# Moving the small arithmetic of a normalisation from VectorE to GpSimd in a two-image convolution kernel

## The reference

```python
x = x + _L0_conv_ref(_gn(x))       # a two-sided cosine transform of the normalised image
x = x + _L1_conv_ref(_gn(x), ...)  # six Euler steps of an ODE

def odefunc(t, y):
    h = relu(_group_norm(y, gn1_w, gn1_b))
    h = _concat_conv(t, h, conv1_w, conv1_b)     # 3x3, 33 channels in, 32 out
    h = relu(_group_norm(h, gn2_w, gn2_b))
    h = _concat_conv(t, h, conv2_w, conv2_b)
    return _group_norm(h, gn3_w, gn3_b)
# six times: y = y + dt * odefunc(t, y)
```

## Time and profile before

| what | us |
|---|---|
| median of 3 runs | 3509.87 |
| lowest and highest | 3505.09, 3530.72 |
| the profiled execution, own time | 3496.76 |
| its span in the trace | 3494.9 |
| TensorE busy | 2976.7 |
| VectorE busy | 2722.9 |
| ScalarE busy | 2497.4 |
| GpSimd busy | 891.2 |

### The profile page before, as it was taken

How to read it: one execution, slowest core, us unless ns; L and a number is a source line. 1 busy time by engine, 2 the same in 40 slices (tenths; PEclk the granted TensorE clock), 3 DMA queues, 4 the chain that set the end, 5 groups by cost and what they waited for, 6 DMA issues and landing times.

```text
span 3494.9 us, 148263 instructions
## 1 busy us (share of the span) xinstructions
PE 2976.7 (85%) x61716; PEld 2505.7 (72%) x61716; DVE 2722.9 (78%) x6289; ACT 2497.4 (71%) x3867; POOL 891.2 (25%) x1293
## 2 busy tenths in 40 slices
PE   2599988989889998899889988889888989888884
PEld 2487777777777776777777777777776777777773
DVE  6588876887778787788877887688876887768883
ACT  0377778777786677767786776877778677787774
POOL 4034311332123221323212331133311432111111
PEclk9699999999999999999999999999999999999997
DMA  4300133113131230331314113221133113231014
GB/s 88 84 22 21 28 51 96 49 55 83 26 96 50 91 69 3 96 95 49 67 26 118 49 49 67 59 86 49 54 62 96 49 49 86 30 95 58 31 49 111
DMA packets 370208, 217.56 MB, mean 62 GB/s; under 512 B 354544, under 2 KB 354912, under 8 KB 367456
## 3 DMA queue, kind: packets, MB, share of 16 engines
q1 hardware_dynamic: 369504, 207.64, 23.7%
HBM read 104.85 MB, written 77.07 MB: 52 GB/s over the span
## 4 chain that ended last, share of the span: by engine, by line
issue 27%; PE 22%; DVE 21%; ACT 20%; POOL 4%; DMA 3%; SPq 3%; DVEq 0%; POOLq 0%; ACTq 0%
PE cps L1468 17%; ACT z L706 7%; ACT z L676 6%; DVE y L1104 3%; DVE unread_yz L1112 3%; SPq L443 2%; ACT hb L705 2%; ACT unread_z L696 2%; DVE ha L1100 2%; DVE bnt L1130 2%; PE dps L1584 2%; DMA y<-xa 2%; PE dps L1576 2%; ACT ha L705 1%; ACT y L769 1%
## 5 line engine op out<-in xcount | busy, mean ns | idle before, releaser
L1468 PE MATMUL cps<-ha,w 64*64 64x392 f16 (+1 forms) x27648 | 1373.6, 341 | 99.3 <-DVE ha L1100 68.3
L1468 PE MATMUL cps<-hb,w 64*64 64x392 f16 x27648 | 1289.8, 335 | 41.1 <-DVE hb L1100 14.6
L1468 PEld LDWEIGHTS cps<-ha,w 64*64 64x64 f16 x27648 | 1064.7, 108 | 282.5 <-issue 132.2
L676 ACT ACTIVATE z<-cps,bias_now 128x784 f32<-128x784 f32 (+2 forms) x1056 | 764.2, 739 | 652.5 <-PE cps L1468 643.0
L1468 PEld LDWEIGHTS cps<-hb,w 64*64 64x64 f16 x27648 | 1077.3, 108 | 155.6 <-issue 49.5
L513 POOL TENSOR_TENSOR small<-small,half 128x1 f32<-128x1 f32 x304 | 168.7, 555 | 1758.1 <-DVE small L1029 1224.3
L1130 DVE BATCH_NORM_STATS2 bnt<-z 128x6 f32<-128x392 f32 (+1 forms) x768 | 389.9, 551 | 149.9 <-ACT z L676 149.4
L1100 DVE TENSOR_TENSOR ha<-z,ha 128x784 f16<-128x784 f32 x384 | 383.4, 998 | 86.5 <-ACT z L706 79.2
L1100 DVE TENSOR_TENSOR hb<-z,hb 128x784 f16<-128x784 f32 x384 | 375.1, 977 | 85.7 <-ACT z L706 76.8
L706 ACT ACTIVATE z<-z,small 128x784 f32<-128x784 f32 x384 | 396.5, 1033 | 1.6
L1104 DVE SCALAR_TENSOR_TENSOR y<-z,small,y 128x784 f32<-128x784 f32 x384 | 397.6, 1038 | 0.1
(11 more groups left out here) (162 smaller groups left out, 2667.8 us busy)
## 6 DMA issues: line engine op xcount, KB each, us to landing
xa<-x_dram SPq DMA_DIRECT2D x128, 196.0 KB, 5.1
y<-xa SPq DMA_DIRECT2D x16, 1568.0 KB, 7.5
y_dram<-y SPq DMA_DIRECT2D x128, 196.0 KB, 4.7
x_dram<-x1s SPq DMA_DIRECT2D x30, 784.0 KB, 5.3
fin<-y_dram SPq DMA_DIRECT2D x30, 784.0 KB, 7.4
xs<-in_x_dram SPq DMA_DIRECT2D x116, 196.0 KB, 4.4
fin<-x_dram SPq DMA_DIRECT2D x28, 784.0 KB, 6.1
out_dram<-fin SPq DMA_DIRECT2D x28, 784.0 KB, 3.6
```

Source lines behind the costliest of these rows:

```text
L676: return nc.scalar.activation(dst, src, ACT.Identity, bias=bias_now[parts, conv:conv + 1], **more)
L1468: return pe.matmul(dst, w[hin * 64:(hin + 1) * 64, kx, a, wl, :], src[:, :, 0:NA], start=(what == "X" and n == 0), stop=(what == "Y" and n ...
```

## The change

For Z1 of both slots and all kinds of steps, ScalarE now copies the sums out of PSUM (`first_read`), and GpSimd does all small operations in `first_post`: seven, each waiting for the one before. For the next image, GpSimd does the seven operations of `next_pre` and the four of `next_post`, with ScalarE's `half_read` between. VectorE does nothing for them any more. Beside this, operations stand at other places: the batches of the next image's statistics, `last_add` (from phase 3 to behind the second product of phase 1), the first `added` (ahead of slot 1's update and not inside it), ScalarE's last activation of slot 1 (behind the last squares), and on TensorE the next image's statistics matmul, from (5, 0) to (3, 0) of phase 1, and those of Z2, from (1, 3) to (1, 5) in phase 2 and from (1, 5) to (2, 1), or to (2, 0) where the step isn't MID, in phase 3.

```diff
 POSTS = {
-    MID: [(Z1, 0), (Z1, 1), (Z2, 0), (Y, 0), (Z2, 1), (Y, 1)],
-    FOUR: [(Z1, 0), (Z1, 1), (Z2, 0), (Y, 0), (Z2, 1), (Y, 1), (IZ, 0)],
-    FIVE: [(Z1, 0), (IZ, 1), (Z1, 1), (IY, 0), (Z2, 0), (IY, 1), (Z2, 1)],
-    LAST_MID: [(Z1, 0), (Z1, 1), (Z2, 0), (Y, 0), (Z2, 1), (Y, 1)],
-    LAST: [(Z1, 0), (Z1, 1), (Z2, 0), (Z2, 1)],
+    MID: [(Z2, 0), (Y, 0), (Z2, 1), (Y, 1)],
+    FOUR: [(Z2, 0), (Y, 0), (Z2, 1), (Y, 1), (IZ, 0)],
+    FIVE: [(IZ, 1), (IY, 0), (Z2, 0), (IY, 1), (Z2, 1)],
+    LAST_MID: [(Z2, 0), (Y, 0), (Z2, 1), (Y, 1)],
+    LAST: [(Z2, 0), (Z2, 1)],
...
+            def first_post(slot, ev, n):
+
+                def at(k):
+                    return col(small, slot, Z1, k)
+
+                done = NFIRST * n
+                pool.wait_ge(stat_read, ev + 2)
+                nc.gpsimd.tensor_tensor(at(T1), at(MS), at(MS), ALU.mult).then_inc(first_done, 1)
+                pool.wait_ge(first_done, done + 1)
+                nc.gpsimd.tensor_tensor(at(VAR), at(ES), at(T1), ALU.subtract).then_inc(first_done, 1)
+                pool.wait_ge(first_done, done + 2)
+                pool.sem_inc(pool_gate, 1)
+                nc.gpsimd.tensor_scalar(at(VE), at(VAR), 0.0, gb[:, 6:7], ALU.max, ALU.add).then_inc(first_done, 1)
+                pool.wait_ge(first_done, done + 3)
+                nc.gpsimd.tensor_tensor(at(RSTD), at(VE), half[:, 0:1], ALU.pow).then_inc(first_done, 1)
+                pool.wait_ge(first_done, done + 4)
+                nc.gpsimd.tensor_tensor(at(SC), at(RSTD), gb[:, 2:3], ALU.mult).then_inc(first_done, 1)
+                pool.wait_ge(first_done, done + 5)
+                nc.gpsimd.tensor_tensor(at(T2), at(MS), at(SC), ALU.mult).then_inc(first_done, 1)
+                pool.wait_ge(first_done, done + 6)
+                nc.gpsimd.tensor_tensor(at(BI), gb[:, 3:4], at(T2), ALU.subtract).then_inc(first_done, 1)
+                pool.wait_ge(first_done, done + 7)
...
-                pool.wait_ge(pow_done, pows)
                 pool.wait_ge(lo_done, NP * c + 1)
...
+            def next_pre(n):
+
+                b = NHALF_STEPS * n
+                pool.wait_ge(s_m0, b + 1)
+                me, ve, mo, vo = (bn0[:, :, k] for k in (1, 2, 4, 5))
+                nc.gpsimd.tensor_tensor(m0[:, 0, 0:CQ], me, mo, ALU.add).then_inc(s_m0, 1)
+                nc.gpsimd.tensor_tensor(m0[:, 1, 0:CQ], ve, vo, ALU.add).then_inc(s_m0, 1)
+                nc.gpsimd.tensor_tensor(m0[:, 1, CQ:2 * CQ], me, me, ALU.mult).then_inc(s_m0, 1)
+                nc.gpsimd.tensor_tensor(m0[:, 5, 0:CQ], mo, mo, ALU.mult).then_inc(s_m0, 1)
+                pool.wait_ge(s_m0, b + 5)
+                nc.gpsimd.tensor_tensor(m0[:, 5, CQ:2 * CQ], m0[:, 5, 0:CQ], m0[:, 1, CQ:2 * CQ], ALU.add
+                                        ).then_inc(s_m0, 1)
+                pool.wait_ge(s_m0, b + 6)
+                pool.sem_inc(pool_gate, 1)
+                nc.gpsimd.tensor_scalar(m0[:, 7, 0:CQ], m0[:, 1, 0:CQ], 2.0 / H, None, ALU.mult).then_inc(s_scaled, 1)
+                pool.wait_ge(s_scaled, n - HALVES + 1)
+                nc.gpsimd.tensor_tensor(m0[:, 0, CQ:2 * CQ], m0[:, 7, 0:CQ], m0[:, 5, CQ:2 * CQ], ALU.add
+                                        ).then_inc(s_m0, 1)
+
+            def next_post(n, ev):
+                b = NHALF_STEPS * n
+                pool.wait_ge(stat_read, ev + 2)
+                nc.gpsimd.tensor_tensor(m0[:, 3, 0:CQ], m0[:, 2, 0:CQ], m0[:, 2, 0:CQ], ALU.mult).then_inc(s_m0, 1)
+                pool.sem_inc(pool_gate, 1)
+                nc.gpsimd.tensor_scalar(m0[:, 6, 0:CQ], m0[:, 2, 0:CQ], -1.0, None, ALU.mult).then_inc(s_m0, 1)
+                pool.wait_ge(s_m0, b + 9)
+                nc.gpsimd.tensor_tensor(m0[:, 4, CQ:2 * CQ], m0[:, 2, CQ:2 * CQ], m0[:, 3, 0:CQ], ALU.subtract
+                                        ).then_inc(s_m0, 1)
+                pool.wait_ge(s_m0, b + 10)
+                pool.sem_inc(pool_gate, 1)
+                nc.gpsimd.tensor_scalar(m0[:, 3, CQ:2 * CQ], m0[:, 4, CQ:2 * CQ], 0.0, EPS, ALU.max, ALU.add
+                                        ).then_inc(s_m0, 1)
...
-                pows = rsqrt_of(Z1, 0)
-                wrap_rows(0, conv_at(g, s, 1), fixes, pows)
+                stats = stats_before(g, s, kind)
+                hn = HALVES * (g + 1) + s
+                first_post(0, stats + STATS[kind].index((Z1, 0)), fixes)
+                wrap_rows(0, conv_at(g, s, 1), fixes)
                 if kind == FIVE:
                     rsqrt_of(IZ, 1)
-                pows = rsqrt_of(Z1, 1)
-                wrap_rows(1, conv_at(g, s, 2), fixes + 1, pows)
                 if kind == MID:
-                    half_rsqrt(HALVES * (g + 1) + s, m0)
-                    half_bias(HALVES * (g + 1) + s)
+                    next_pre(hn)
+                first_post(1, stats + STATS[kind].index((Z1, 1)), fixes + 1)
+                if kind == MID:
+                    next_post(hn, stats + STATS[MID].index((X0, 0)))
+                wrap_rows(1, conv_at(g, s, 2), fixes + 1)
+                if kind == MID:
+                    half_rsqrt(hn, m0)
+                    half_bias(hn)
...
+            def first_read(slot, ev):
+
+                act.wait_ge(stat_done, ev + 1)
+                nc.scalar.activation(col(small, slot, Z1, MS, 2), sps[:, 0:2], ACT.Identity).then_inc(stat_read, 1)
+
+            def half_read(ev):
+
+                act.wait_ge(stat_done, ev + 1)
+                nc.scalar.activation(m0[:, 2, :], sps[0:H, 0:2 * CQ], ACT.Identity).then_inc(stat_read, 1)
...
+                first_read(0, stats_before(g, s, kind) + STATS[kind].index((Z1, 0)))
                 evacuate(1, 0, s, 0, 0, c)
-                act.wait_ge(post_done, posted(Z1, 0))
+                act.wait_ge(first_done, NFIRST * (2 * (STEPS * g + s) + 1))
                 activate(0, Z1, 0)
...
+                first_read(1, stats_before(g, s, kind) + STATS[kind].index((Z1, 1)))
                 evacuate(0, 1, s, 1, 0, c)
-                act.wait_ge(post_done, posted(Z1, 1))
+                if kind == MID:
+                    half_read(stats_before(g, s, kind) + STATS[MID].index((X0, 0)))
+                act.wait_ge(first_done, NFIRST * (2 * (STEPS * g + s) + 2))
                 activate(1, Z1, 0, False)
                 squares(0, 0, c, sq + 0)
                 activate(1, Z1, 1, False)
                 activate(1, Z1, 2, False)
                 squares(0, 1, c, sq + 1)
                 evacuate(0, 1, s, 1, 2, c)
+                squares(0, 2, c, sq + 2)
+                evacuate(0, 1, s, 1, 3, c)
+                squares(0, 3, c, sq + 3)
                 activate(1, Z1, 3, False)
-                evacuate(0, 1, s, 1, 3, c)
-                squares(0, 2, c, sq + 2)
-                squares(0, 3, c, sq + 3)
                 if kind == FIVE:
                     start_squares(1, SLOTS * (g + 1) + 1, HALVES * (g + 1) + 1)
...
-                if early:
-                    early()
...
                 pre_of(Z1, 0, 9)
                 if kind == MID:
                     half_batch(0, hn)
-                post_of(Z1, 0)
+                    half_batch(1, hn)
                 stats_of(0, 0)
                 split_for(1, 0)
                 if kind == MID:
-                    half_batch(1, hn)
+                    half_batch(2, hn)
                 split_for(1, 1)
                 stats_of(0, 1)
-                if kind == MID:
-                    half_batch(2, hn)
                 if kind == FIVE:
                     start_stats(1, g + 1, range(7))
                     dve.wait_ge(ibn_done, SLOTS * (g + 1) + 2)
                     pre_of(IZ, 1, 7)
                 split_for(1, 2)
                 stats_of(0, 2)
+                if kind == MID:
+                    half_batch(3, hn)
                 stats_of(0, 3)
 
                 dve.wait_ge(bn_done, 2 + 2 * u)
                 if kind == FIVE:
                     post_of(IZ, 1)
                 split_for(1, 3)
-                post_of(Z1, 1, meanwhile=(lambda: half_batch(3, hn)) if kind == MID else None)
-                if kind == MID:
-                    half_pre(hn)
                 dve.wait_ge(y_new[0], 16 * (g + 1))
                 dve.wait_ge(y_new[1], 16 * (g + 1))
                 products_of(1, 0)
                 split_for(2, 0)
                 split_for(2, 1)
-                if kind == MID:
-                    half_post(hn, stats_before(g, s, kind) + STATS[MID].index((X0, 0)))
                 if kind == FIVE:
                     post_of(IY, 0)
                 if kind == FOUR:
                     start_stats(0, g + 1, (0, 1, 2))
                 products_of(1, 1)
+                if kind == MID:
+                    with dve.If(g > 0):
+                        last_add(g * HALVES + s)
+                if adds:
+                    last_add(g * HALVES + s)
                 split_for(2, 2)
...
-                update(1, lambda: euler(1, 0), (lambda: added(0)) if kind == MID else None)
```

(13 more changed lines are left out.)

11 lines of the change are left out of this document (7 added, 4 removed).

## The result

The changed kernel takes 3566.91 us (median of 4 runs, 3564.59 to 3572.52), the kernel before 3507.48 beside it (4 runs): ratio 1.0184, interval 1.0143 to 1.0225. The change makes the kernel 1.8% slower. The forecast of 3655 had the sign and held the time in its range, but made the loss more than twice too large: +148 against +68 between the two profiled executions (3496.76 and 3564.59).

What follows compares the result with a forecast made beforehand. TensorE's convolutions (85% busy) set the pace where not held up, largely by VectorE. MID steps gave 99 and 3, FOUR and FIVE 28, the last group 18: +148, stated as 3655 us, range 3475 to 3740.

Steps and rivals of the forecast that it cites:

- (a): MID step, slot 0: GpSimd's chain of 3.36 us and ScalarE's read of 0.5 start its activation 1.5 us late.
- (b): MID step, slot 1's statistics: the next image's fourth batch adds 0.5 us, so their matmul is 2.0 late.
- (c): MID step, slot 1: GpSimd's queue and chain make its first activation 4.6 us late (3.6 to 6.8).
- (d): MID step, VectorE before the update: next image's part out, final addition in, +1.0 us less 0.1; phase 3 5.5 late.
- (e): MID step, phase 3: of 4.0 us of TensorE stalls 3.0 are left, so -1.0 us (0 to -4.0).
- The queue in (c): Ahead of slot 1's chain in a MID step: the next image's seven GpSimd operations take 4.0 us, delaying it 1.1.
- the sign that the prediction named: A TensorE stall of about half a microsecond at the next image's statistics matmul, which would show the forecast right.
- the rival of the ports: GpSimd's chains held up by VectorE splits or products on shared ports, 0.6 us or more each: 3697 us, chance 0.16.
- The six first steps: First steps of six groups: the late chain hides behind the state's DMA wait, 0.5 us each counted, 3 in all.
- Faster: GpSimd operations as quick as VectorE's (0.22), slot 1's activation 1.5 late, phase 3 returns 4.0: 3440 us, chance 0.21.
- Given back: Low ends everywhere and phase 3 returns all 4.0 us; a MID step changes by only 0.5: 3530 us, chance 0.12.
- The clock: TensorE's granted clock falls after some 6 us of stalls in each of 28 MID steps: 3728 us, chance 0.12.

Runs made afterwards that it cites:

- e6: Changed kernel with slot 1's first normalisation arithmetic back on VectorE, slot 0's still on GpSimd: 3515.24 us, ratio 1.0042 to the kernel before.
- e9: Changed kernel with four more dependent plain 128x1 GpSimd operations, results unused, at the head of slot 1's chain: 3624.29 us, ratio 1.0344 to the kernel before.
- e12: Kernel before with last_add behind the fourth split of phase 4 and only the first normalisation on GpSimd: 3539.20 us, ratio 1.0113.
- e1: Changed kernel with ScalarE's last activation of slot 1 again ahead of the evacuation of pair 3 and squares 2 and 3: 3564.94 us, ratio 1.0169.
- e2: Changed kernel with last_add back in phase 3, behind the third split of phase 4: 3592.46 us, ratio 1.0244 to the kernel before.
- e4: Changed kernel with the first normalisation's arithmetic of both slots back on VectorE, all else kept: 3498.77 us, ratio 0.9997 to the kernel before.
- e8: Kernel before with only last_add moved, to behind the fourth split of phase 4 and the addition b=2: 3471.60 us, ratio 0.9898.

## Why the prediction was right in sign and wrong in size

By its own steps, forecast against the step of 748.75 to 818.68:

| step | forecast | measured |
|---|---|---|
| (a) slot 0's activation late | 1.5 | 0.36 |
| (b) further, to slot 1's statistics | 0.5 | 0.40 |
| (c) further, to slot 1's activation | 2.6 | 1.25 |
| (d) further, to the update and phase 3 | 0.9 | 0.62 |
| (e) phase 3 gives back | -1.0 | -0.97 |
| MID step | +4.5 | +1.66 |

**The step that failed is the price in (a), which is also the price in (c).** "A plain 128x1 operation costs between 0.35 ... and 0.54", and 0.40 was taken; it is 0.19. The chain was put at 3.36 and takes 2.43; ScalarE's read with its handovers was put at 0.5 and takes 743.03 - 742.78 = 0.25. The mechanism (each chain longer, slot 1's without cover, the delay carried by VectorE's order to phase 3) is what e6, e9 and e12 show. The two bounds were the mistake. The lower one took the power on 128x1 (0.54) and subtracted one column at the slope of 0.19; this charges every plain operation with whatever a power costs once. The upper one was the product of 112x16 that took 0.54: in the kernel after, the same form takes 0.21 to 0.23 where VectorE does no operation with two inputs beside it. That 0.54, from 750.23 to 750.77, stood beside a product of VectorE that ran to 750.69:

```profile
749.72 0.97 DVE L1112 SCALAR_TENSOR_TENSOR unread_yz<-z,y 128x784 bf16<-128x784 f32 x1
```

The memset of 0.19 was in the text, as a bound for another term, and was the right row.

**The queue in (c) doesn't exist.** It followed from the same price: seven operations in 4.0 us, where they take 754.83 to 756.68 = 1.85. No stall stands at the next image's statistics matmul, against the sign that the prediction named. Of the 1.25 of (c), 0.7 is the last operation beside VectorE's product. That was the rival of the ports: its 0.6 was near, though only 30 of 48 chains of slot 1 pay it, and it is part of a sum that was too large elsewhere. The Trainium skill (SBUF — State Buffer, "SBUF: two separate sides", the reading of the diagram) says that the pair of ports which the two engines share goes to whichever starts first, for its whole instruction, where VectorE has two inputs in SBUF and GpSimd reads SBUF, and that the other is blocked; the trace agrees, since the operation of 759.61 ends at 760.52 and the product beside it at 760.48.

(b), (d) and (e) were right within 0.3. In (e) that is not only the number: the columns' new stall was forecast at 1.3 and is 1.20, that of the third group of rows at 1.3 and is 1.39, and the 1.93 went. In (d) the addition of 1.8 in phase 1 is partly hidden, since the update waits there for ScalarE's last activation too: with the order back (e1) and without the addition (the first group) a step falls by 1.1, and either alone brings nothing at full clock. e2 shows that phase 1 was nevertheless the better place, so the 1.93 that went was worth more than what came.

**Outside the MID steps.** 22 steps of 4.5 made 99; with 1.66 they would be 37, and 33.2 were measured. That the two are so near is luck: four steps of the first group lost 3.45 each, since they had no stall of 1.93 to win back, and the 18 lost 1.08, made small by the clock of the kernel before. Errors are left that partly cancel. FOUR and FIVE lost 32.9, forecast 28, although the chain was late by less: nothing returns there (e4 gives back 2.4 and 2.0 a step). The last group lost 11.9, forecast 18. The six first steps gained 14.3 where 3 was to be lost. That gain isn't the first normalisation's, since e4 keeps it (72.89), and it goes with the clock. In the kernel before, the two first steps with a granted clock of 0.98 take 72.5 and 73.0, as all six do in the changed kernel (71.3 to 73.4 at 0.98 and 1.00); the four others have 0.91 to 0.95 and take 74.2 to 77.4. As an estimate, 0.05 of the clock over 77 us is 3.9, nearly the whole difference. e8 (71.0 to 71.8 at 0.98, 74.0 to 75.2 below) splits in the same way. Why the changed kernel keeps the clock there, and the kernel before doesn't, stays open.

**The rivals.** "Faster" had the right price (0.22) and the right place of slot 1's activation (1.5 late forecast, 2.0 measured), and by its own rule that decides below 3.1. It failed by its other half, that phase 3 returns all 4.0 us. The forecast had that right. The time lies between the two because each had one of the terms. "Given back" (3530) needed the 4.0 as well. The clock is not the cause of the loss: the mean granted clock is 0.955 in both kernels, steps at a lower clock occur in both, and in the MID steps and the first ones it favours the changed kernel. Two neighbouring steps of the changed kernel, of which the second, at 0.98, is a microsecond longer (columns as for e8):

```profile
748.75:818.68 69.93, 62.69 (x1315) 51.38 (x1309) 55.56 (x121) 50.92 (x84) 29.16 (x56) 1.00 0.19 60
818.68:889.64 70.96, 64.27 (x1315) 52.27 (x1309) 53.73 (x111) 50.69 (x84) 27.85 (x55) 0.98 0.16 45
```

## What to carry to other kernels

A chain of small dependent operations belongs on the engine that does it soonest, not on the one that is idle: VectorE, busy for three quarters of the time, with 2.66 us from statistics to activation beat GpSimd, busy for a third, with 3.95, and each microsecond more of a chain that has no cover costs a microsecond in a step (e9). Price a small operation by a row near to it that stands alone (here a memset), not by a difference between two others, and look what the neighbour engine did beside a row before it becomes a bound. Before arithmetic is moved off an engine to make room, look where that engine's own gaps are: one addition, moved by one split into a gap of 1.8 us, gave 1%, which the whole change didn't. Before two mean step times are compared, sort the steps by granted clock: here four slow steps of one kernel hid a third of the difference.

## What the runs showed of the hardware that was not expected

- GpSimd on one column (128x1, f32): a product or sum of two tensors 0.19, one with two constants 0.31, a power 0.56; 0.27 from start to start of dependent ones. On 16 columns (112x16) a product or sum is 0.21 to 0.23, a power 3.4 to 3.7. So the first 15 columns more cost a plain operation under 0.04, a power 3.
- A GpSimd operation that starts beside a VectorE operation with two inputs in SBUF is not over before that operation is: 0.91 in place of 0.19, and in e9 1.38 in place of 0.57, of which VectorE's product covers the first 0.96. In the changed kernel's trace 94 small products and sums of GpSimd start within a split or product of VectorE of about 0.98, and none ends more than 0.05 before it.
- ScalarE reads 128x2 from PSUM in 0.17, as fast as VectorE's copy (0.16).
